# Four sums of the first weight set, two of them moved from GpSimd to VectorE, and the gates' tanh moved behind the casts

## The reference

```python
x = x + tanh(g_xattn) * xattn(layernorm(x), ctx, mask, w_q, w_k, w_v, w_o, q_norm_w, k_norm_w)
x = x + tanh(g_ffn) * ffn(layernorm(x), A, B, Wr)
# xattn: q = h @ w_q.T (32 heads of 128), k = ctx @ w_k.T and v = ctx @ w_v.T (8 heads of 128),
#        rmsnorm of q and k, softmax(q k / sqrt(128) + mask) @ v, then @ w_o.T
# ffn:   scores = h @ Wr.T, softmax over the 16 best of 64 experts as gates,
#        out = sum over experts of gate * (h @ A.T) @ B.T
```

## Time and profile before

| | us |
|---|---|
| median of 3 runs | 2381.99 |
| lowest and highest of them | 2379.24, 2382.4 |
| the profiled execution, its own time | 2379.71 |
| its span, first to last instruction | 2377.9 |
| TensorE busy, of the span | 2278.4 (96%) |
| VectorE busy | 1611.9 (68%) |
| GpSimd busy | 1317.3 (55%) |
| ScalarE busy | 1172.6 (49%) |
| mean granted TensorE clock | 0.989 |

### The profile page before, as it was taken

How to read it: one execution, slowest core, us unless ns; L and a number is a source line. 1 busy time by engine, 2 the same in 40 slices (tenths; PEclk the granted TensorE clock), 3 DMA queues, 4 the chain that set the end, 5 groups by cost and what they waited for, 6 DMA issues and landing times.

```text
span 2377.9 us, 35655 instructions
## 1 busy us (share of the span) xinstructions
PE 2278.4 (96%) x11600; PEld 1911.7 (80%) x11600; DVE 1611.9 (68%) x2649; ACT 1172.6 (49%) x3751; POOL 1317.3 (55%) x1823
## 2 busy tenths in 40 slices
PE   5998999999999989999999899899899999999899
PEld 4886887888888878888888788688687787788687
DVE  6557557777777797777777845755756877544755
ACT  4546546666666676666666722422423334332421
POOL 5566668655565566555555645554655765434321
PEclk8999999999999999999999999999999999999999
DMA  4687556757757457642222545555456466324643
GB/s 170 217 228 268 187 159 231 216 163 198 197 165 198 131 193 195 194 126 89 89 93 95 191 165 177 203 180 202 151 168 238 142 210 253 121 72 144 228 169 133
DMA packets 180231, 412.98 MB, mean 174 GB/s; under 512 B 12176, under 2 KB 77968, under 8 KB 164624
## 3 DMA queue, kind: packets, MB, share of 16 engines
q1 hardware_dynamic: 175440, 379.24, 46.6%
q0 software_dynamic: 4608, 31.46, 7.4%
HBM read 293.21 MB, written 178.26 MB: 198 GB/s over the span
## 4 chain that ended last, share of the span: by engine, by line
PE 86%; POOL 4%; issue 3%; DVE 3%; DMA 3%; ACT 1%; SPq 0%; POOLq 0%; ACTq 0%; DVEq 0%
PE bank L715 24%; PE bank L717 23%; PE bank L716 23%; PE bank L773 4%; PE bank L781 2%; PE bank L761 2%; PE bank L798 1%; PE bank L797 1%; PE bank L796 1%; DVE t_lo L1239 1%; DMA staged<-heads 1%; POOL staged L1696 1%; POOL s_hi L1706 1%; DMA staged<-in_w_q 1%; PE bank L813 1%
## 5 line engine op out<-in xcount | busy, mean ns | idle before, releaser
L715 PE MATMUL bank<-t_hi,s_hi 128*128 128x512 f32 x2688 | 1091.3, 406 | 81.1 <-issue 42.7
L717 PE MATMUL bank<-t_hi,s_lo 128*128 128x512 f32 x2688 | 1059.3, 394 | 0.0
L716 PE MATMUL bank<-t_lo,s_hi 128*128 128x512 f32 x2688 | 1056.1, 393 | 0.0
L715 PEld LDWEIGHTS bank<-t_hi,s_hi 128*128 128x128 f32 x2688 | 510.3, 190 | 189.0 <-issue 85.4
L1239 DVE TENSOR_TENSOR s_lo<-staged,s_hi 128x512 fp32r<-128x512 f32 x672 | 538.2, 846 | 99.6 <-ACT s_hi L962 92.0
L717 PEld LDWEIGHTS bank<-t_hi,s_lo 128*128 128x128 f32 x2688 | 508.8, 189 | 112.0
L716 PEld LDWEIGHTS bank<-t_lo,s_hi 128*128 128x128 f32 x2688 | 510.9, 190 | 91.0
L962 ACT CAST s_hi<-staged 128x512 fp32r<-128x512 f32 x434 | 250.2, 623 | 342.7 <-DMA staged<-heads 181.0
L1679 POOL TENSOR_SCALAR small<-small 128x4 f32<-128x4 f32 (+1 forms) x192 | 66.3, 345 | 414.5 <-ACT small L1051 338.4
L1694 POOL TENSOR_TENSOR staged<-staged 128x512 f32<-128x512 f32 x96 | 139.3, 1451 | 271.1 <-DMA staged<-heads 97.6
L1239 DVE TENSOR_TENSOR t_lo<-t_raw,t_hi 128x2048 fp32r<-128x2048 f32 x70 | 183.2, 2625 | 34.2 <-ACT t_hi L951 25.1
(11 more groups left out here) (131 smaller groups left out, 2961.7 us busy)
## 6 DMA issues: line engine op xcount, KB each, us to landing
heads<-heads SPq DMA_DIRECT2D x128, 256.0 KB, 3.7
t_raw<-combos SPq DMA_DIRECT2D x28, 1024.0 KB, 10.2
t_raw<-in_sets SPq DMA_DIRECT2D x25, 1024.0 KB, 9.6
staged<-in_w_q SPq DMA_DIRECT2D x32, 768.0 KB, 5.9
staged<-heads SPq DMA_DIRECT2D x32, 768.0 KB, 5.9
sums<-sums SPq DMA_DIRECT2D x18, 1024.0 KB, 7.9
sums<-sums SPq DMA_DIRECT2D x36, 512.0 KB, 4.6
xt<-x_columns SPq DMA_DIRECT2D x8, 1792.0 KB, 7.2
```

Source lines behind the costliest of these rows:

```text
L715: nc.tensor.matmul(out, s_hi[w][:, cols], high, start=start, stop=False, skip_group_check=True)
L716: nc.tensor.matmul(out, s_hi[w][:, cols], low, start=False, stop=False, skip_group_check=True)
L717: done = nc.tensor.matmul(out, s_lo[w][:, cols], high, start=False, stop=at == 3, skip_group_check=True)
```

## The change

All four sums are made by VectorE. `t_raw[1]` is made between `t_lo[2]` and `t_lo[3]`, `t_raw[6]` between `t_lo[3]` and `t_lo[1]`. GpSimd's start holds only `sums(0)`. On VectorE `first_t(6)`, `kw` and `tg2` move from the start into entry 0, behind `third_product`. On ScalarE the wait for the constants, the two tanh and the load of the table with exp and ln move behind the last cast of the set, and the wait for `kw` moves to `key_columns(0, ...)`, which uses it.

```diff
@@ ScalarE, key_columns
             act.wait_ge(kt_done, 2 * e + w + 1)
+            if e == 0:
+                act.wait_ge(kw_set, 1)
@@ ScalarE, first_t
-            elif k in (2, 3):
-                act.wait_ge(t0_combo, k - 1)
             else:
-                act.wait_ge(t0_combo_pool, 1 if k == 1 else 2)
+                act.wait_ge(t0_combo, {2: 1, 3: 2, 1: 3, 6: 4}[k])
@@ ScalarE, start
         first_t(2)
         first_t(3)
+        first_t(1)
+        first_t(5)
+        first_t(6)
         act.wait_ge(const_in, 16 * CONSTS)
         nc.scalar.activation(tgx[:, :], gates_in[:, 0:1], ACT.Tanh).then_inc(gate_tanh, 1)
         nc.scalar.activation(tgf[:, :], gates_in[:, 1:2], ACT.Tanh).then_inc(gate_tanh, 1)
         act.preload_act_table_set("natural_log_exp_and_others")
-        first_t(1)
-        first_t(5)
-        first_t(6)
-        act.wait_ge(kw_set, 1)
@@ VectorE, first_t
-            if k == 3:
-                dve.wait_ge(t0_combo_pool, 1)
-            if k == 1:
-                dve.wait_ge(t0_combo_pool, 2)
+            if k in (1, 3):
+                dve.wait_ge(t0_combo, 4 if k == 1 else 3)
@@ VectorE, start
         first_t(2)
+        dve.wait_ge(t0_combo, 2)
+        nc.vector.tensor_tensor(t_raw[1][:, :, :], t_raw[3][:, :, :], b11_again[:, :, :], ALU.add).then_inc(t0_combo, 1)
         first_t(3)
-        dve.wait_ge(const_in, 16 * CONSTS)
-        nc.vector.tensor_scalar(kw[:, :], nw[:, 0:1], nw[:, 1:2], ...).then_inc(kw_set, 1)
-        dve.wait_ge(gate_tanh, 2)
-        nc.vector.tensor_scalar(tg2[:, :], tgf[:, :], 2.0, None, ALU.mult).then_inc(gate_set, 1)
+        dve.wait_ge(again_in[1], 16)
+        dve.wait_ge(t0_combo, 3)
+        nc.vector.tensor_tensor(t_raw[6][:, :, :], b21_again[:, :, :], t_raw[1][:, :, :], ALU.add).then_inc(t0_combo, 1)
         first_t(1)
         first_t(5)
-        first_t(6)
@@ VectorE, entry loop
                 if j == 2:
                     third_product(e)
+                    if e == 0:
+                        first_t(6)
+                        dve.wait_ge(const_in, 16 * CONSTS)
+                        nc.vector.tensor_scalar(kw[:, :], ...).then_inc(kw_set, 1)
+                        dve.wait_ge(gate_tanh, 2)
+                        nc.vector.tensor_scalar(tg2[:, :], ...).then_inc(gate_set, 1)
@@ GpSimd, start
         sums(0)
-        pool.wait_ge(t0_combo, 2)
-        pool.wait_ge(again_in[0], 16)
-        nc.gpsimd.tensor_tensor(t_raw[1][:, :, :], t_raw[3][:, :, :], b11_again[:, :, :], ALU.add).then_inc(t0_combo_pool, 1)
-        pool.wait_ge(again_in[1], 16)
-        pool.wait_ge(t0_combo_pool, 1)
-        nc.gpsimd.tensor_tensor(t_raw[6][:, :, :], b21_again[:, :, :], t_raw[1][:, :, :], ALU.add).then_inc(t0_combo_pool, 1)
```

More of the change, by code:

```diff
@@ L307, in program @@
     again_in, b12_in = [sem(f"again_in{w}") for w in range(2)], sem("b12_in")
-    t_hi_done, t_lo_done, t0_combo, t0_combo_pool = sem("t_hi_done"), sem("t_lo_done"), sem("t0_combo"), sem("t0_combo_pool")
+    t_hi_done, t_lo_done, t0_combo = sem("t_hi_done"), sem("t_lo_done"), sem("t0_combo")
     st_in, st12_in = sem("staged_in"), sem("staged12_in")
@@ L1528, in _ @@
         first_t(2)
+        dve.wait_ge(t0_combo, 2)
+        nc.vector.tensor_tensor(t_raw[1][:, :, :], t_raw[3][:, :, :], b11_again[:, :, :], ALU.add).then_inc(t0_combo, 1)
         first_t(3)
-        dve.wait_ge(const_in, 16 * CONSTS)
-        nc.vector.tensor_scalar(kw[:, :], nw[:, 0:1], nw[:, 1:2], float(HEAD_DIM) ** -0.5, ALU.mult, ALU.mult).then_inc(kw_set, 1)
-        dve.wait_ge(gate_tanh, 2)
-        nc.vector.tensor_scalar(tg2[:, :], tgf[:, :], 2.0, None, ALU.mult).then_inc(gate_set, 1)
+        dve.wait_ge(again_in[1], 16)
+        dve.wait_ge(t0_combo, 3)
+        nc.vector.tensor_tensor(t_raw[6][:, :, :], b21_again[:, :, :], t_raw[1][:, :, :], ALU.add).then_inc(t0_combo, 1)
         first_t(1)
         first_t(5)
-        first_t(6)
         for e in range(KV0, QA0):
@@ L1545, in _ @@
                     third_product(e)
+                    if e == 0:
+                        first_t(6)
+                        dve.wait_ge(const_in, 16 * CONSTS)
+                        nc.vector.tensor_scalar(kw[:, :], nw[:, 0:1], nw[:, 1:2], float(HEAD_DIM) ** -0.5, ALU.mult, ALU.mult).then_inc(kw_set, 1)
+                        dve.wait_ge(gate_tanh, 2)
+                        nc.vector.tensor_scalar(tg2[:, :], tgf[:, :], 2.0, None, ALU.mult).then_inc(gate_set, 1)
                 if j == 3:
```

## The result

| | before | after |
|---|---|---|
| median, us (runs) | 2381.99 (9) | 2373.95 (9) |
| lowest, highest | 2378.55, 2384.92 | 2371.69, 2375.82 |
| the profiled execution, its time | 2379.71 | 2372.72 |
| its span | 2377.9 | 2370.9 |
| granted clock, mean | 0.989 | 0.991 |

The ratio of after to before is 0.997, 95% interval 0.9961 to 0.9979: 5.0 to 9.3 us faster. The medians are 8.0 us apart, the two profiled executions 7.0.

A forecast was written before the change was run, and what follows sets the result against it. TensorE bounds the kernel and runs unbroken from entry 1 on, so only entry 1's start counts. Starting at 49.0 to 50.3 against 54.89 gains 5.3 us: 2381.99 - 5.3 = 2376.7 us, range 2373.0 to 2380.0.

The forecast's parts named there:

- Added waits at nothing: On VectorE: waits for its own earlier results, another instruction in between each time, and for a long-issued load, cost nothing.
- Collision: From 27.2 on, GpSimd's staging sums take turns with VectorE's instructions: three turns of 1.08, 3.2 us in all.
- Product 3: On TensorE: starts at 29.6 in place of 32.00, runs at the higher clock for 3.0 us, ends at 32.6.
- the rival with GpSimd first: At 27.2 GpSimd goes first: low halves from product 3 on 1.08 later, gain 3.5 to 4.8, 2377.8 us; chance 0.25.
- Product 1: On TensorE: starts at 36.15 behind a 3.6 us wait, takes 5.46 us as product 3 did before, ends at 41.6.
- the rival with the higher clock: Product 1 stays at the higher clock: gain 8.1, or 7.0 with GpSimd first, 2373.9 to 2375.0 us; chance 0.22.
- X: The start of product 5 on TensorE, forecast at 43.2; entry 1 follows 5.75 to 7.1 us later.
- ScalarE: Moving ScalarE's tanh and table load behind the last casts costs nothing; without that cover 1.7 us.
- The sum: Entry 1 starts at 49.0 to 50.3 against 54.89: gain 4.6 to 5.9, taken as 5.3 us; chance 0.35.
- No gain: Each turn on the shared port costs VectorE 1.8 us more than the 1.08 counted: 2382.0 us; chance 0.06.
- VectorE keeps its turn: VectorE issues back to back, shutting GpSimd out until 36.1: gain 10.5, 2371.5 us; chance 0.05.
- Slower by the clock: At later set changes two that kept TensorE's clock lose it, 7.0 us against 5.3: 2383.7 us; chance 0.07.

The follow-up runs named there:

- repeat_after: The changed kernel run and profiled once more with no edit; median 2373.87 us, ratio 0.9963 to before.
- busy_pe: The changed kernel with idle-time matmuls, results unread, ahead of products 2, 3, 1 and 5 of entry 0; median 2374.34 us, ratio 0.9973 to before.
- tanh_back: The changed kernel with ScalarE's constants, tanh and table load back ahead of the casts of products 1, 5 and 6; median 2372.83 us, ratio 0.9965 to before.
- low6_first: The changed kernel with the low half of product 6 made ahead of usum again; median 2374.76 us, ratio 0.9976 to before.
- late_sums: The changed kernel with GpSimd's staging sums of entry 1 waiting until product 6's low half is made; median 2370.34 us, ratio 0.9951 to before.

## Why the prediction was right, point by point

- **What bounds.** Right for the gain that the traces show: it was made before entry 1, and what moved it later, the repeats of before show as well. Whether the times hold a little more is the open end below.
- **Added waits at nothing.** Wrong. I wrote that another instruction lay between each new wait and what it waits for. The low half of product 3 waits for the sum straight ahead of it, and the low half of product 1 too. So it starts when that sum has ended, at 27.37 and not 27.22. The wait itself costs 0.1 to 0.15 us. In two traces it also let GpSimd in, at a price of 1.03: without a gap VectorE goes on 2.2 us after an instruction's start, which would be 27.28 in repeat_after and 27.36 in busy_pe (an estimate from the starts of their sums, 25.08 and 25.16), and GpSimd's first staging sum came at 27.36 and 27.42. In after it came at 27.17 and in tanh_back at 26.79, ahead of that moment. There GpSimd would by its arrival have been first without the gap too, as it was between low halves in a row. In low6_first it came at 27.55, too late for the gap.
- **Collision.** The mechanism, the alternation and its price were right: 1.03 us a turn measured, 1.08 taken. The number of turns was four, not three: 4.1 us in place of 3.2. In VectorE's line the low half of product 5 ended at 40.49 in place of 39.34.
- **Product 3** started at 30.77, as under the rival with GpSimd first (30.7). Not seen by me: product 2 ran at the lower clock and ended at 30.7, just in time, so that the 2.5 us which the lower clock cost it delayed nothing.
- **Product 1** began at 37.34 in place of 36.15, but took 4.57 us in place of 5.46, since it began at the higher clock. The two errors nearly cancel, which is luck: its end at 41.91 against 41.6. In repeat_after it took 3.0 us and X was 42.20; that is the rival with the higher clock and GpSimd first, a gain of 7.0 forecast and 6.9 measured. It ran at the higher clock throughout in one of three traces with this opening (repeat_after, not after or tanh_back), which doesn't contradict the 0.22 I gave it and is too few to confirm it.
- **X** = 43.58 against 43.2, then entry 1 5.82 later against 5.75. The wait for bank 3 was there: TensorE went on to product 6 at 46.56, 2.98 us after product 5's start (3.0).
- **ScalarE** at nothing: right, and shown by tanh_back.
- **The sum** at entry 1: 5.49 against 5.3 in this trace, 6.9 in the next. The likeliest case was not what happened: it was GpSimd first, whose middle gain of 4.2 was too low by the 0.9 us of product 1, less 0.2 for starts that came later than its own, and by 0.6 because product 5 kept the higher clock throughout.
- **From the gain to the time.** 8.0 us by the medians, 5.3 forecast. The time, 2373.95, lies within the range of 2373.0 to 2380.0 but below the forecast's own 2375.0 to 2378.5; the number alone would have pointed to the rival with the higher clock (2373.9 to 2375.0), which the profiled execution wasn't. The profiled execution of before was among its better ones: its repeats lost 1.3 to 2.8 us more at the first changes of set, and one of them had it back at the end. Some 1.4 us between 5.5 and 6.9 at entry 2 is the clock of product 1. The openings alone (5.5 to 6.9) lie in the interval of 5.0 to 9.3; the larger sample, 7.9 give or take 1.1, excludes 5.5 as the whole gain but not 6.9. Whether a further 1 to 2 us is won behind the opening, and by what, stays open.
- **No gain**: refuted; a turn cost VectorE 1.03 us, not 1.8 more than the 1.08 (three times 1.8 is 5.4, not 5.3). By the rule of the Trainium skill (Perfetto Trace Analysis, Optimizing Scalar/DVE Operations) the move might not have helped. What it warns of was there, and late_sums measured it as 4.1 us on VectorE's line and 3.1 to 4.5 at entry 2, some half to four fifths of what the change brought. Moving the work helped because 4.4 us on GpSimd became 2.2 on VectorE.
- **VectorE keeps its turn**: refuted by every trace with both at work. **Slower by the clock**: such steps are real: 1.3 us at entry 10 with the clock, up to 3.0 at entry 90, against 3.5 each in the rival. The largest net loss after the opening, 5.3 us in busy_pe, still left a lead. None of the changed kernels came out slower than before.

## What to carry over

When work leaves one of two engines that take turns, look at what the freed engine does next: here its next job moved forward onto the same stretch and took back some half to four fifths of what the change won, and one wait that held it back for 14 us was worth a further 3.5 us (2370.34 against 2373.87 in the same round). A wait for one's own last result leaves a gap in which the other engine can get in (in repeat_after it came 0.03 us ahead), and an engine that already waits gets its turn without a gap. And judge an edit of the opening by the lead at the first repeated event behind it, then by many runs: single traces of one kernel drift apart by 3 us at the end.

## What I had not expected of the hardware

- The turns go strictly to whoever is first, at the grain of one instruction: 27.17 against 27.37 in after, 27.36 against 27.39 in repeat_after and 27.55 against 27.42 in low6_first, so 0.03 to 0.2 us in arrival, decide whether VectorE stands for 1.0 to 1.1 us or GpSimd for 2.0.
- TensorE's clock after the same wait isn't the same each time. Behind 3.3 to 3.6 us the first matmuls of product 1 ran at 1.00 in after (0.47 us for the first) and in repeat_after, and it then fell within the product in after, but not in repeat_after. Behind 3.75 us in the earlier trace rows it was 0.50 from the start. The length of the wait alone doesn't decide it: in tanh_back product 1 began at the lower clock behind 2.08 us (0.74 us for the first matmul).
- The opening of the kernel before was the same to 0.11 us in three executions that differ in TensorE's clock, while whole executions differ by 3 us. That scatter is made near the changes of set, and the part of it at entry 10, 1.3 us, goes with the clock of that stretch (1.00 or 0.93 to 0.94).
